# A wait after each ten gathers of the first tile, on those ten

## The reference

```python
item_id_feat = item_table[item_id]                       # 2048 x 128
item_img_feat = gelu(ln(item_emb_d128 @ mm_w + mm_b))
target = item_id_feat + item_img_feat
seq_emb = item_table[item_seq]                           # 2048 x 50 x 128
x = concat([t, seq_emb, t - seq_emb, t * seq_emb])       # t: target, repeated 50 times
scores = relu(x @ aw1 + ab1) @ aw2 + ab2                 # masked where item_seq == 0
hist_feat = einsum('bs,bsd->bd', softmax(scores), seq_emb)
sparse = stack([like_feat, view_feat, item_id_feat, item_img_feat, hist_feat])
se = sparse * gate(sparse)                               # a small squeeze-and-excite gate
dnn_in = concat([se, bilinear pairs of se])              # 15 features of 128
for i in range(2):
    xc = dnn_in * (xc @ cross_K[i] + cross_bias[i]) + xc # cross_K[i] is 1920 x 1920
h = gelu(ln(xc @ w1 + b1)); h = gelu(ln(h @ w2 + b2))
return sigmoid(h @ w3 + b3)
```

## Time and profile before

| | |
|---|---|
| time, median of 3 runs | 2131.74 us (2131.51 to 2133.45) |
| the profiled execution | 2132.89 us, of which the span from first to last instruction 2131.0 us |
| granted TensorE clock, mean | 0.942 |
| PE busy | 1931.2 us (91%) |
| PE weight loads busy | 1517.0 us (71%) |
| DVE busy | 1333.2 us (63%) |
| ACT busy | 903.4 us (42%) |
| POOL busy | 900.5 us (42%), 800 gathers into `e` among it |

### The profile page before, as it was taken

One profiled execution on the slowest core, in us unless ns is written; L12 is line 12 of the kernel. 1 busy time (PEld: TensorE's weight loads), 2 busy tenths in 40 slices (PEclk: granted clock), 3 DMA queues, 4 the chain that ended last, 5 costly groups with the idle time before them and its releaser, 6 DMA issues. The chain is left out here.

```text
span 2131.0 us, 32802 instructions
## 1 busy us (share of the span) xinstructions
PE 1931.2 (91%) x9608; PEld 1517.0 (71%) x9608; DVE 1333.2 (63%) x2213; ACT 903.4 (42%) x1963; POOL 900.5 (42%) x854
## 2 busy tenths in 40 slices
PE   2656557999999999999999999999999999999997
PEld 1444335777777887767777887777777888888885
DVE  3555554666777766667777756667777754445553
ACT  1433342445445344664445335654445333322223
POOL 7777775566655521556555501646550000000000
PEclk6866667999999999999999999999999999999998
DMA  5111113334333462334333452334433352333330
GB/s 161 51 49 53 49 46 85 98 109 126 117 111 116 125 210 74 100 88 132 117 106 118 142 184 71 102 89 127 123 104 92 106 179 81 88 98 99 95 90 20
DMA packets 99535, 220.31 MB, mean 103 GB/s; under 512 B 21648, under 2 KB 27040, under 8 KB 99232
## 3 DMA queue, kind: packets, MB, share of 16 engines
q1 hardware_dynamic: 62928, 136.90, 21.3%
q0 software_dynamic: 27136, 55.63, 10.4%
q10 hardware_dynamic: 9296, 25.70, 3.2%
HBM read 205.29 MB, written 12.85 MB: 102 GB/s over the span
## 5 line engine op out<-in xcount | busy, mean ns | idle before, releaser
L394 POOL DMA_INDIRECT e<-in_item_table,idx_all x800 | 848.2, 1060 | 658.8 <-issue 310.3
L1090 DVE TENSOR_TENSOR Wl<-raw,Wh 128x640 fp32r<-128x640 f32 (+1 forms) x420 | 337.9, 805 | 295.6 <-DVEq L1089 294.3
L774 ACT ACTIVATE Wh<-raw 128x640 fp32r<-128x640 f32 (+1 forms) x420 | 301.7, 722 | 503.1 <-ACTq L773 497.0
L522 PE MATMUL xps<-X0h,Wh 128*128 128x512 f32 x900 | 364.7, 405 | 6.7 <-PEq L520 6.7
L522 PE MATMUL xps<-X1h,Wh 128*128 128x512 f32 x900 | 360.2, 400 | 0.0
L524 PE MATMUL xps<-X0h,Wl 128*128 128x512 f32 x900 | 352.2, 391 | 0.0
L523 PE MATMUL xps<-X0l,Wh 128*128 128x512 f32 x900 | 351.9, 391 | 0.0
L524 PE MATMUL xps<-X1h,Wl 128*128 128x512 f32 x900 | 351.4, 390 | 0.0
L523 PE MATMUL xps<-X1l,Wh 128*128 128x512 f32 x900 | 351.3, 390 | 0.0
L737 ACT ACTIVATE e<-e,pw 128x128 f32<-128x128 f32 x800 | 242.7, 388 | 15.5 <-ACTq L128 15.5
L522 PEld LDWEIGHTS xps<-X0h,Wh 128*128 128x128 f32 x900 | 169.9, 189 | 40.8 <-issue 8.6
(11 more groups left out here) (144 smaller groups left out, 2213.7 us busy)
## 6 DMA issues: line engine op xcount, KB each, us to landing
raw<-in_cross_K SPq DMA_DIRECT2D x360, 320.0 KB, 2.9
raw<-in_w SPq DMA_DIRECT2D x60, 256.0 KB, 2.7
e<-in_item_table,idx_all POOLq DMA_INDIRECT x800
dnn_scratch<-dn ACTq DMA_DIRECT2D x12, 960.0 KB, 4.7
x1f<-dnn_scratch ACTq DMA_DIRECT2D x3, 2048.0 KB, 9.8
x1f<-dnn_scratch ACTq DMA_DIRECT2D x3, 1792.0 KB, 15.5
dn<-in_embT SPq DMA_DIRECT2D x1, 1024.0 KB, 5.3
img_scratch<-dn ACTq DMA_DIRECT2D x1, 1024.0 KB, 4.6
```

The costliest lines, as they stand in the source:

```text
L394: nc.gpsimd.indirect_dma_start(out=dst, out_offset=None, in_=table, in_offset=bass.IndirectOffsetOnAxis(ap=idx_all[:, t, s:s + 1], axis=0) ...
L522: m0 = mm(out, wh, Xh[:, 0:T, k, :], start=(k == 0), stop=False)
L774: af(Wh[:, split_slot(w), 0:n], raw[:, rs, 0:n], ACT.Copy).then_inc(hi_done, 1)
L1090: v.tensor_tensor(Wl[:, rs, 0:n], raw[:, rs, 0:n], Wh[:, slot, 0:n].bitcast(F32), ALU.subtract).then_inc(lo_done, 1)
```

## The change

One wait of the opening is made another one for tile 0. After the ten gathers of each group of tile 0, group 0 too, POOL waits until these ten have landed. Tiles 1 to 3 keep the wait for the group ahead, and tiles 4 to 15 their waits on fives.

```diff
                         if t >= TILES[0] and (s + 1) % SUB == 0:
 
                             pool.wait_ge(e_landed[g], (t * GRP + s + 1 - g * GRP) * DMA)
-                    if t < TILES[0] and g:
+                    if t == 0:
+
+                        pool.wait_ge(e_landed[g], DMA * GRP)
+                    elif t < TILES[0] and g:
 
                         pool.wait_ge(e_landed[g - 1], (t + 1) * (DMA * GRP))
```

## The result

The changed kernel takes 2142.54 us in the median (five runs, 2139.47 to 2144.11) against 2131.92 us of before (five runs, 2131.51 to 2133.45). The measured ratio of the two kernels' times is 1.0043, with a 95% interval of 1.0031 to 1.0054: 9.2 us slower, 6.6 to 11.5. The two medians lie 10.6 us apart. The profiled execution took 2139.47 us, with a span of 2137.6 us.

The account below looks back on a forecast made before the run. POOL's gathers and their landing bound the opening, matmuls the rest. Five waits add 8.4 us; replayed with DVE's delays and the store, tile 1 is 7.9 us late: 2131.74 + 7.9 = 2139.6 us, range 2138.0 to 2142.1 us.

Parts of the forecast that it names:

- Where it is paid: Opening: a POOL delay reaching tile 1's first gather is paid in full at the program's end; forecast 7.9 us.
- rival that hides it in tile 0: Tile 0: PE begins late and POOL's lead lasts, so nothing changes: 2131.7 us; chance 0.04.
- The price of a wait: Tile 0's five waits: 1.8 us behind groups 0, 2, 3 and 2.25 us behind 1, 4, against 0.30 us gaps.
- the replay: Tile 0's gathers re-timed at 1.25 us each, delayed by DVE instructions with two SBUF inputs: tile 1 starts at 89.3 us.
- the rival of five such waits: Tile 0: each of the five waits costs 3.70 us, 17 us in all, 2148.7 us; chance 0.13.
- The bare sum: Tile 0's five waits above their 0.30 us gaps, before DVE's effect: 3 x 1.5 + 2 x 1.95 = 8.4 us.
- What DVE gives back: Tile 0: DVE instructions with two SBUF inputs delay gathers anyway, absorbing some lateness; 8.4 us of waits become 7.9 us.
- the replay of group 2: Tile 0, group 2: starts at 45.15 us, fifth gather at 50.15 us delayed to 51.41 us, ends at 57.65 us.
- That DVE's times stay: Tile 0: DVE's times up to 67 us stay unchanged, as groups 0 to 2 landed long before PE came.
- The hold d of group 4: Tile 0, group 4: DVE's fourth L994 delays a gather by 0.24 to 1.49 us; 0.85 us taken.
- Phase in tiles 1 to 3: Rival: shifted gathers meet DVE's instructions better, saving 7.6 us of 15.2 us, ending at 2132.0 us; chance 0.08.
- The rest of the program as long as before: Behind the first product: length unchanged; a changed length would show the prediction wrong.

Follow-up runs that it names:

- the fives: Tile 0 waits after every five gathers for these, ten waits in all, against the kernel before: median 2150.29 us, ratio 1.0079 (1.0066 to 1.0093).

## Why the prediction was right, and what it mis-sized

- **Where it is paid.** Right. POOL's delay at tile 1 reached the first product (9.96 us, then 9.15 us), and no rival that hides it in tile 0 has a run for it: PE waited 5.28 us for tile 1's group 0. That the time came out at 9.2 us, nearer to the forecast of 7.9 us than the 9.96 us at tile 1, is in part luck: tiles 1 to 3 took 0.8 us less, which the next points show to be within their scatter.
- **The price of a wait.** Right. 1.8 us for one semaphore was measured as 1.98, 1.80 and 1.77 us, 2.25 us for the last as 2.48 us, and the one beside the store cost 3.60 us where the replay had 3.3 us. In the other two profiles with the five waits the first cost 2.27 and 2.20 us, the others 1.75 to 1.92 us and 2.29 to 2.34 us. Only the wait beside the store came near 3.70 us, so the rival of five such waits has no run for it; in the fives one of the added waits did cost 3.87 us, in the middle of group 0, while the first loads of the cross layers' weights were on the DMA queues. The bare sum, 9.5 us with the store, was measured as 10.1 us. The Trainium skill (DMA: Bandwidth & Descriptors, Anatomy of one DMA) gives a DMA a fixed cost of about 2.0 us, most of it the wait until the last byte is confirmed as landed. The idle times here, counted from the end of the gather's 0.94 us on POOL and without the one beside the store, are 1.77 to 2.48 us.
- **What DVE gives back.** Right in mechanism, wrong in size: the term that took 1.6 us off the bare sum was measured as 0.2 us at tile 1's first gather (10.1 us of waits, 9.96 us late). Group 1's hold was met as replayed: its gathers ended at 30.72 and 33.15 us, and the tenth started at 37.21 us. The step that failed is the replay of group 2. It let the fourth gather, at 48.90 us, through just ahead of DVE's product, which it kept at its old 49.10 us. The gather came at 49.25 us, since the waits behind groups 0 and 1 brought it 0.35 us later than forecast, and the product came at 48.82 us, 0.28 us earlier than the earlier trace rows, as the next rows of the changed kernel show. By the replay's own arithmetic either of the two would have been enough for the hold. That DVE's times stay was wrong too for group 2, whose product came at 64.69 us, 1.5 us earlier.

```profile
48.82 1.49 DVE L997 TENSOR_TENSOR teT<-eT,tT 128x1280 f32<-128x1280 f32 x1 [2.65 <-DVEq L996]
...
57.63 1.49 DVE L997 TENSOR_TENSOR teT<-eT,tT 128x1280 f32<-128x1280 f32 x1 [2.07 <-DVEq L996]
...
64.69 1.49 DVE L997 TENSOR_TENSOR teT<-eT,tT 128x1280 f32<-128x1280 f32 x1 [2.07 <-DVEq L996]
```

 With the gather at 49.25 us held, group 2's last gather came to 57.68 us, just behind the start of the next product, was held to 59.93 us, and its wait began only then. Group 3 started at 61.74 us in place of 59.45 us and ended at 74.48 us in place of 72.22 us. That is the slip by one more gather that the forecast's own range allowed for. The hold d of group 4 was mis-sized the other way: 0.85 us were taken, and the fourth product cost 0.19 us (the gather at 81.25 us) and the instruction at 87.26 us 0.28 us. Its bounds of 0.24 to 1.49 us don't follow from the rows either: a held gather ends 0.82 us after the instruction and takes 0.94 us anyhow, so they would be 0.12 to 1.37 us, and before the product of that group cost 0.15 us.
- **Phase in tiles 1 to 3.** The argument against this rival, that DVE follows POOL and both keep their phase, was too strong. The holds of the same program differed by 1.8 us between two profiles, and first products by 4.2 us. In the changed kernel tiles 1 to 3 took 0.8 us less than before. So the rival is real as a scatter of some microseconds, and not as the cause of the change's time.
- **The rest of the program as long as before.** Wrong by 2.55 us in both profiles of the changed kernel, and the prediction had named this as a sign of being wrong. But this part runs the same program in all kernels here, and in their profiles it took 1789.6 to 1792.8 us; the kernel with the wait behind group 1 had 1790.6 and 1792.4 us in its two. So the 2.55 us are not shown to come from the change. Of the changed kernel's runs the profiled executions were the shortest, in both sets of five. The other runs, 1 to 5 us longer, have no profile; where their time lies stays open, and whether the slower median (10.6 us) is more than the ratio's 9.2 us can't be told.

## What to carry to other kernels

A wait for transfers just issued costs their landing, each time, in the queue that issues them; whether the program pays is decided by whether that queue bounds the stage, and in an opening that it bounds everything behind is late by the sum. Price such waits from places where the kernel already waits so, look at what else is on the DMA engines at each, and don't count on holds by other engines to swallow the delay: their phase shifts by tenths of a microsecond and a whole step of the stream goes with it. When the issuing engine is the bound, look first at what lengthens its instructions: here one input moved from SBUF to PSUM on another engine was worth more than the waits.

## What the runs showed that was not expected

- DVE's product of 1280 columns with both inputs in SBUF held gathers on POOL up to 1.3 us each; with one input in PSUM it held none, and the mean gather fell from 1046 to 965 ns. The Trainium skill (SBUF — State Buffer, Who interferes with whom) has the rule for two SBUF inputs against a GpSimd instruction that reads SBUF; this run bears it out for gathers by an index in SBUF.
- A gather that starts just behind the issue of a 1 MB store on another queue made the wait behind it cost 4.42 us, one that ended just ahead of it 2.36 us. The latter was ahead of it since a gather some 7 us earlier had escaped a hold by 0.05 us.
- In the first 10 us of products the granted clock averaged 0.85 in the changed kernel, with 38 matmuls begun, and 0.75 before, with 34; both rose to 1.00 (2.4 GHz) in the 10 us behind it. In both PE had waited 6.69 us just before. Four matmuls more, at 0.2 us each (1757 us for 8784), are by estimate 0.8 us of the 2.55 us by which the matmul part was shorter. These are the windows, after and before:

```profile
347.95:357.95 10.00, 10.00 (x38) 8.15 (x39) 1.65 (x2) 2.37 (x4) 4.97 (x6) 0.85 0.24 67
```

```profile
338.80:348.80 10.00, 10.00 (x34) 7.99 (x35) 1.65 (x2) 1.75 (x3) 6.10 (x7) 0.75 0.25 69
```
